# Interaction tower on one core: gathered rows turned by DMAs instead of on TensorE, sums in smaller groups, and a table load that waits piece by piece

## What is computed

```python
e = jnp.stack([tbl_f[ids[:, f]] for f in range(32)], axis=1)      # 2048 x 32 x 64
z = jnp.sum(e, axis=-1)
outer = jnp.einsum('bpd,pde,bpe->bp', e[:, II, :], kernels, e[:, JJ, :])
h = jnp.concatenate([z, outer, dense_ctx], axis=1)
h = jnp.maximum(h @ W_top1 + b_top1, 0.0)
h = jnp.maximum(h @ W_top2 + b_top2, 0.0)
y = h @ W_top3
```

## Time and profile before

| | |
|---|---|
| median of 3 runs (range) | 1235.91 us (1235.64 to 1238.09) |
| the profiled execution | 1238.17 us |
| its span, first to last instruction | 1236.4 us |
| TensorE matmul busy | 1074.5 us, 87% |
| VectorE (DVE) busy | 628.0 us, 51% |
| ScalarE (ACT) busy | 142.5 us, 12% |
| GpSimd (POOL) busy | 483.8 us, 39% |
| mean granted TensorE clock | 0.945 of full speed |

### The profile page before, as it was taken

One profiled execution on the slowest core, in us unless ns is written; L12 is line 12 of the kernel. 1 busy time (PEld: TensorE's weight loads), 2 busy tenths in 40 slices (PEclk: granted clock), 3 DMA queues, 4 the chain that ended last, 5 costly groups with the idle time before them and its releaser, 6 DMA issues.

```text
span 1236.4 us, 30329 instructions
## 1 busy us (share of the span) xinstructions
PE 1074.5 (87%) x13964; PEld 460.2 (37%) x13964; DVE 628.0 (51%) x658; ACT 142.5 (12%) x219; POOL 483.8 (39%) x518
## 2 busy tenths in 40 slices
PE   1565737898989888999999999989998999999998
PEld 0453614343334233334343443333343343333333
DVE  0331412264546353656665654556664655589880
ACT  0100110101001101201010021210020020210101
POOL 7444373325543443454445433354445423400000
PEclk9877768899989789999999999999999999999999
DMA  9100010001010000010010000000011000000000
GB/s 335 38 17 18 16 26 13 15 11 21 19 22 12 16 17 14 15 21 18 17 20 20 18 13 13 15 19 19 19 19 20 19 10 15 16 3 2 3 3 0
DMA packets 24376, 29.24 MB, mean 24 GB/s; under 512 B 13366, under 2 KB 13624, under 8 KB 24123
## 3 DMA queue, kind: packets, MB, share of 16 engines
q0 software_dynamic: 16384, 16.81, 7.0%
q1 hardware_dynamic: 7856, 10.49, 2.5%
q10 hardware_dynamic: 10, 0.01, 0.0%
HBM read 27.27 MB, written 0.01 MB: 22 GB/s over the span
## 4 chain that ended last, share of the span: by engine, by line
PE 85%; issue 11%; DVE 1%; another core or an unknown queue 1%; DMA 1%; POOL 1%; ACT 0%; DVEq 0%; ACTq 0%; POOLq 0%
PE y L631 48%; PE accs L649 25%; PE y L611 3%; PE y L710 2%; PE y L693 2%; PE y L681 2%; DVE prod L576 1%; PE y L686 1%; PE y L723 1%; POOL rows L384 1%; DMA rows<-tbl,ids_sb 0%; ACT xt L430 0%; PE y L662 0%; DMA ids_sb<-ids 0%
## 5 line engine op out<-in xcount | busy, mean ns | idle before, releaser
L576 DVE TENSOR_TENSOR prod<-y,xt 128x1024 f32<-128x1024 f32 (+3 forms) x570 | 587.5, 1080 | 561.9 <-PE y L631 373.3
L384 POOL DMA_INDIRECT rows<-tbl,ids_sb x512 | 483.1, 944 | 597.3 <-DVE prod L576 309.2
L631 PE MATMUL y<-xt,kw 64*32 64x512 f32 (+2 forms) x8432 | 647.8, 560 | 66.9 <-issue 53.0
L649 PE MATMUL accs<-prod,ones_strip 64*32 64x512 f32 (+2 forms) x4960 | 352.5, 526 | 67.5 <-issue 66.6
L631 PEld LDWEIGHTS y<-xt,kw 64*32 64x32 f32 (+1 forms) x8432 | 236.8, 115 | 422.5 <-issue 384.4
L649 PEld LDWEIGHTS accs<-prod,ones_strip 64*32 64x32 f32 x4960 | 149.0, 112 | 232.2 <-issue 208.2
L430 ACT COPY xt<-y 128x1024 f32<-128x1024 f32 (+2 forms) x48 | 34.9, 728 | 608.0 <-PE y L611 513.0
L611 PE MATMUL y<-ident,rows 128*128 128x128 f32 x256 | 42.3, 289 | 21.4 <-DMA rows<-tbl,ids_sb 16.2
L548 DVE TENSOR_REDUCE z_rows<-rows 128x8 f32<-128x512 f32 (+2 forms) x80 | 42.9, 570 | 15.2 <-DMA rows<-tbl,ids_sb 15.2
L611 PEld LDWEIGHTS y<-ident,rows 128*128 128x128 f32 x256 | 28.7, 142 | 49.8 <-issue 42.7
L461 ACT COPY h_in<-accs 128x1024 f32<-128x1024 f32 (+2 forms) x10 | 8.4, 842 | 221.1 <-PE accs L649 141.4
(11 more groups left out here) (22 smaller groups left out, 67.5 us busy)
## 6 DMA issues: line engine op xcount, KB each, us to landing
rows<-tbl,ids_sb POOLq DMA_INDIRECT x512
kw<-pair_k SPq DMA_DIRECT2D x14, 512.0 KB
w_sb<-w SPq DMA_DIRECT2D x1, 1024.0 KB
w_sb<-w SPq DMA_DIRECT2D x1, 512.0 KB
kw<-pair_k SPq DMA_DIRECT2D x1, 384.0 KB
kw<-pair_k SPq DMA_DIRECT2D x1, 256.0 KB, 4.1
w1z_sb<-w1z SPq DMA_DIRECT2D x1, 256.0 KB
ids_sb<-ids SPq DMA_DIRECT2D x1, 240.0 KB, 2.7
```

The lines of the kernel that those rows point to most:

```text
L384: pool.indirect_dma_start(out=rows[:, s, c, h, :], out_offset=None, in_=tables[f], in_offset=bass.IndirectOffsetOnAxis(ap=ids_sb[:, b, f:f ...
L576: nc.vector.tensor_tensor(prod_part(t, d, n), y_part(t, d, n), x, ALU.mult).then_inc(y_read, n)
L631: last = nc.tensor.matmul(y[columns, h, :], kw[part, d, columns], xt[part, slot_of(t, units[h][0] // 2), 0:w], start=True, stop=True)
L649: last = nc.tensor.matmul(accs[32 * q:32 * q + 32, n, 0:w], ones_strip[part, STRIPS - 1 - s:2 * STRIPS - 1 - s], prod_part(t, u // 2)[part ...
```

## The change

It has three parts.

**Rows turned by DMAs.** In tiles 1 to 4 TensorE no longer transposes. A float32 is two 16-bit halves. ACT copies a couple's gathered rows apart into low and high halves (`split_rows`, new buffer `split`), SP issues one transposing DMA for the couple from `split` to `halves`, and ACT copies the halves together into `xt` (`join_halves`). The transposing DMAs go one at a time, and two couples can be on the way. `join_at` and `split_at` take the place of `visits`: a couple is joined three full steps before the first step that needs it and at least 2.5 before the next couple's join, and split five full steps ahead of its join. Gathers start 48 full steps ahead of the split. A row slot is free when the couple has been split and summed. To make room, `xt` has 18 slots instead of 20 and `h2` lies in `h1`. Tile 0 is turned on TensorE as before. The dense columns go through ACT's queue into one of two buffers, and the field sums are turned at step 108 of each tile instead of 76.

**Sums.** Groups are two `prod` slots, four groups are in flight, and sums go two groups behind.

**The table.** Each of the 17 DMAs waits until the one before it has landed (the first six), later until the one before that has.

```diff
-XT_SLOTS = 20
+XT_SLOTS = 18
+HALF_SLOTS = 2
 FIRST_EXTRA = XT_SLOTS
 EXTRAS = 4
 Y_SLOTS = 3
-GROUP_SLOTS = [4] * TILES
+GROUP_SLOTS = [2] * TILES
+PROD_GROUPS = 4
+SUM_LAG = 2
...
+K_ALONE = 6
...
-def visits_ahead(t):
-    return {1: [(0, 112), (2, 116)], 2: [(0, 100), (2, 112)]}.get(t, [(0, 84), (2, 100), (4, 116)])
-def visits(t):
-    early = {1: [(4, 4), (6, 14), (8, 26), (10, 44)], 2: [(4, 2), (6, 12), (8, 24), (10, 40)]}
-    return early.get(t, [(6, 8), (8, 20), (10, 36)]) + [(12, 56), (14, 72)]
+JOIN_MARGIN = 3
+JOIN_SPACING = 2.5
+JOIN_LEAD = 5
+FIRST_SPLITS = [(0, 100), (0, 104), (0, 110), (0, 116), (1, 1), (1, 4), (1, 9), (1, 14), (1, 20)]
+FIRST_JOINS = [(0, 108), (0, 112), (0, 120), (0, 123), (1, 4), (1, 8), (1, 13), (1, 18), (1, 24)]
+def full_steps(t, d):
+    return (N_STEPS * sum(WIDTHS[:t]) + d * WIDTHS[t]) / TILE
+def join_at(t, k):
+    if t == 1 and k < len(FIRST_JOINS):
+        return full_steps(*FIRST_JOINS[k])
+    d = first_step_of_couple(k) if k < COUPLES - 1 else step_at("inner", SETS - 1, 0) - 6
+    at = full_steps(t, d) - JOIN_MARGIN
+    return at if k == COUPLES - 1 else min(at, join_at(t, k + 1) - JOIN_SPACING)
+def split_at(t, k):
+    if t == 1 and k < len(FIRST_SPLITS):
+        return full_steps(*FIRST_SPLITS[k])
+    return join_at(t, k) - JOIN_LEAD
+def moves_of(t):
+    moves = {d: [] for d in range(N_STEPS)}
+    events = [(at(u, k), what, u, k) for u in range(1, TILES) for k in range(COUPLES)
+              for what, at in (("split", split_at), ("join", join_at))]
+    for at, what, u, k in sorted(events):
+        if full_steps(t, 0) <= at < full_steps(t, N_STEPS):
+            moves[int((at - full_steps(t, 0)) * TILE / WIDTHS[t] + 1e-6)].append((what, u, k))
+    return moves
...
-    for k, d in visits(t):
-        work[d // p * p].append(("couples", t, k))
-    work[76].append(("fields", t, 0))
-    if t + 1 < TILES:
-        for k, d in visits_ahead(t + 1):
-            work[d // p * p].append(("couples", t + 1, k))
...
-            if g > 0:
-                order.append(("sum", t, g - 1))
+            if g >= SUM_LAG:
+                order.append(("sum", t, g - SUM_LAG))
             elif t > 0:
-                order.append(("sum", t - 1, len(groups(t - 1)) - 2))
+                order.append(("sum", t - 1, len(groups(t - 1)) - 1 + g - SUM_LAG))
...
-GATHER_LEAD = 56
-STEPS_BEFORE = {}
-_steps = 0
-for _what in PLAN:
-    STEPS_BEFORE[_what] = _steps
-    _steps += _what[0] == "step"
+GATHER_LEAD = 48
...
-    what = Y_ORDER[copy_use(t, k)]
-    goal = FULL_STEPS[STEPS_BEFORE[what]] - GATHER_LEAD + i + 2 * rowsets(t) * (k - what[2])
+    goal = split_at(t, k) - GATHER_LEAD + i
...
+        split = sb("split", [P, HALF_SLOTS, 2 * TILE // P, P], u16)
+        halves = sb("halves", [P, HALF_SLOTS, 2 * TILE // P, P], u16)
...
-        h2 = sb("h2", [P, J2, TILE])
+        h2 = h1[:, 0:J2, :]
...
-            slot = PROD_SLOTS // 2 * (group_number(t, d) % 2) + i // pack(t)
+            slot = GROUP_SLOTS[t] * (group_number(t, d) % PROD_GROUPS) + i // pack(t)
...
-                        pool.wait_ge(y_full, copy_use(*divmod(n - GATHER_SLOTS, COUPLES)) + 1)
+                        before, kb = divmod(n - GATHER_SLOTS, COUPLES)
+                        if before == 0:
+                            pool.wait_ge(y_full, y_use("couple", 0, kb) + 1)
+                        else:
+                            pool.wait_ge(rows_split, move_number(before, kb) + 1)
...
+                if c >= 1:
+                    sp.wait_ge(k_loaded[c - (1 if c < K_ALONE else 2)], 16)
...
-            sp.wait_ge(z_rows_zeroed, 1)
-            for t in range(TILES):
-                if t > 0:
-                    sp.wait_ge(y_full, y_use("fields", t - 1, 0) + 1)
-                for half in range(2):
-                    sp.dma_start(z_rows[:, 0:rowsets(t), half, FIELDS:FIELDS + DENSE],
-                                 dense[:, first_block(t):first_block(t) + rowsets(t), :]).then_inc(dense_loaded, 16)
+            for t in range(1, TILES):
+                for k in range(COUPLES):
+                    i = move_number(t, k)
+                    slot, r = i % HALF_SLOTS, 2 * rowsets(t)
+                    sp.wait_ge(rows_split, i + 1)
+                    if i >= 1:
+                        sp.wait_ge(transposed, 16 * i)
+                    if i >= HALF_SLOTS:
+                        sp.wait_ge(joined, i - HALF_SLOTS + 1)
+                    sp.dma_start_transpose(halves[:, slot, 0:r, :],
+                                           split[:, slot, 0:r, :].rearrange("p c d -> p (c d)")
+                                           ).then_inc(transposed, 16)
...
+            def load_dense(t):
+                for half in range(2):
+                    act.dma_start(z_rows[:, t % 2, 0:rowsets(t), half, FIELDS:FIELDS + DENSE],
+                                  dense[:, first_block(t):first_block(t) + rowsets(t), :]
+                                  ).then_inc(dense_loaded[t % 2], 16)
...
+            def split_rows(t, k):
+                n, i, r = couple(t, k), move_number(t, k), 2 * rowsets(t)
+                words = rows[:, n % GATHER_SLOTS, 0:rowsets(t), :, :].rearrange("p c h d -> p (c h d)").bitcast(u16)
+                act.wait_ge(gathered[n % GATHER_SLOTS], rows_in(n))
+                if i >= HALF_SLOTS:
+                    act.wait_ge(transposed, 16 * (i - HALF_SLOTS + 1))
+                nc.scalar.copy(split[:, i % HALF_SLOTS, 0:r, :].rearrange("p (s c) d -> p s (c d)", s=2),
+                               words.rearrange("p (n s) -> p s n", s=2)).then_inc(rows_split, 1)
+            def join_halves(t, k):
+                n, i, r, w = couple(t, k), move_number(t, k), 2 * rowsets(t), WIDTHS[t]
+                act.wait_ge(transposed, 16 * (i + 1))
+                if n >= XT_SLOTS:
+                    before, kb = divmod(n - XT_SLOTS, COUPLES)
 
                     act.wait_ge(y_read, N_STEPS * before + last_step_of_couple(kb) + 1)
-                s = slot_of(t, k)
-                nc.scalar.copy(xt[:, s:s + count, 0:w], y_banks[u % Y_SLOTS][:, 0:count, 0:w]).then_inc(act_read, 1)
+                nc.scalar.copy(xt[:, slot_of(t, k), 0:w].bitcast(u16).rearrange("p (n s) -> p s n", s=2),
+                               halves[:, i % HALF_SLOTS, 0:r, :].rearrange("p (s c) d -> p s (c d)", s=2)
+                               ).then_inc(joined, 1)
...
-                if g >= 2 and d in groups(t):
-                    dve.wait_ge(summed, g - 1)
+                if g >= PROD_GROUPS and d in groups(t):
+                    dve.wait_ge(summed, g - PROD_GROUPS + 1)
...
-                pe.wait_ge(act_read, copied(t, max(units[0][0], units[1][0]) // 2))
+                k = max(units[0][0], units[1][0]) // 2
+                if t == 0:
+                    pe.wait_ge(act_read, act_uses_through(y_use("couple", 0, k)))
+                else:
+                    pe.wait_ge(joined, move_number(t, k) + 1)
```

More of the change, by code:

```diff
@@ L161, in first_tile_work @@
         work[d // p * p].append(("extra", 0, s))
-    for k, d in visits_ahead(1):
-        work[d].append(("couples", 1, k))
     work[108].append(("fields", 0, 0))
@@ L205 @@
 PLAN = [what for t in range(TILES) for what in plan(t)]
-Y_ORDER = [what for what in PLAN if what[0] not in ("sum", "extra") and (what[0] != "step" or what[2] % pack(what[1]) == 0)]
+Y_ORDER = [what for what in PLAN if what[0] in ("couple", "fields", "mlp1", "mlp2", "mlp3")
+           or what[0] == "step" and what[2] % pack(what[1]) == 0]
 Y_USES = {what: u for u, what in enumerate(Y_ORDER)}
```

104 lines of the change are left out of this document (54 added, 50 removed).

## The result

| | before | changed |
|---|---|---|
| median, range | 1235.86 (1235.64 to 1238.09) | 1257.56 us (1252.67 to 1260.91) |
| ratio, 95% interval | | 1.0165 [1.0144, 1.0185] |
| profiled execution, its span | 1238.17, 1236.4 | 1260.91, 1259.1 us |
| mean granted clock | 0.945 | 0.905 |

Slower by 21.7 us, where the forecast was slower by 7.6.

A forecast was written before the change was run, and what follows sets the result against it. TensorE sets the end, held up by gathers that are cheap spread and dear bunched. 1238.2 - 70.8 + 82 + 0 - 3.6 = 1245.8 us profiled, 1243.5 us median; forecast 1215 to 1275, whole range 1194 to 1296.

The forecast's parts named there:

- transposes leave TensorE: Tiles 1 to 4: turning rows by DMAs takes the transposes off TensorE, -70.8 us, or -56.4 at the lower price.
- gathers bunched: Gathers for tiles 2 to 4: the new order adds 102 back-to-back gathers at 0.80 us each, +82 us.
- smaller groups: Sums: smaller groups keep the step-to-sum distance, move no work and remove a DVE wait that ends last nowhere, 0.
- transposing DMAs: Row turning in tiles 1 to 4: DMAs arrive in time and their traffic is taken as 0, up to +24 us.
- table in pieces: Start of the kernel: loading the table in pieces removes POOL's stand, -3.6 us, with ends 0 and -16.
- 48 x (6.33 - 5.15): Tiles 2 to 4: 48 couples times 1.18 us for eight transposes each on TensorE, 56.6 us.
- rival (3): Tiles bound by gathers: transposes were already paid for in part, 0.94 instead of 1.18 us; 1258 us, within the forecast's 0.48.
- doubled gathers: Gathers sharing a full step with another instead of having their own; 102 more after the change, 0.80 us each.
- with at most two pieces on the way that goes: Tile 0's start: TensorE's stand from 20.05 to 36.22 us behind the table load disappears.
- (1): Gathers: bunching costs less, below 0.73 us per doubled gather, so the kernel is faster; 1202 us at 0.40; chance 0.29.
- (2): Tiles 2 to 4: slow transposing DMAs deliver halves late or their traffic holds up matmuls; 1292 us; chance 0.20.
- tiles 3 and 4 no shorter than before: Sign of being right: these two tiles would not get shorter after the change.

The follow-up runs named there:

- e13: Kernel before with small groups of sums and the changed kernel's gather times in tiles 2 to 4, where before takes 1236.6 to 1237.1: 1267.52 us, 1.0241.
- e4: Kernel before with only the small groups: two product slots, four groups in flight, sums two groups behind: 1210.03 us, 0.9787.
- e16: Changed kernel with 46 of the 64 transposing DMAs replaced by plain 4 KB DMAs, copies, waits and order kept: 1256.94 us, 1.0152.
- e3: Kernel before with only the waits between the 17 DMAs of the table: 1237.06 us, 1.0004.
- e15: Kernel before with small groups of sums and even gather times in tiles 2 to 4, rows turned on TensorE: 1162.37 us, 0.9402.
- e17: Kernel before with only the even gather times in tiles 2 to 4, on a chip where before takes 837.84: 837.49 us, 0.9992.
- e12: Kernel before with small groups and the changed kernel's gather times in tiles 2 to 4, where before takes 837.3 to 837.8: 831.93 us.
- e1: Changed kernel with gathers of tiles 2 to 4 let go evenly, one per full step: 1152.82 us, 0.9325.
- e18: Changed kernel with even gathers six steps earlier and a short POOL MEMSET after each gather of tiles 1 to 4, where before takes 837.84: 881.55 us, 1.0516.

## Why the prediction came out as it did

The direction was right and the time inside the range, but both by luck, and the size was not right: +7.6 us forecast, +21.7 measured, made of three terms that were each off by 24 us or more. By its own terms, on holding chips:

| term | forecast | measured | from |
|---|---|---|---|
| transposes leave TensorE | -70.8 | -9.9, the DMAs and the pieces with it | e13 to changed |
| gathers bunched | +82 | +57.5 | e4 to e13 |
| smaller groups | 0 | -26.5 | before to e4 |
| transposing DMAs | 0 | 0 (0.6) | e16 |
| table in pieces | -3.6 | 0 (+0.5) | e3 |
| sum | +7.6 | +21.1 | the first three |

The three are steps of one path, before to e4 to e13 to changed, so that they add up to the whole is no proof of them; by another path they share it differently.

**The step that failed first is "48 x (6.33 - 5.15)".** The row shows eight transposes, the code says eight *gathers* a couple, and I took the one for the other; a couple of a wide tile has four transposes. The term was 35.4 us at most. With the right count the forecast would have been 1279 us, further off, because the other errors would not have made it up.

**The second is that 1.18 us was carried into cycles with gathers.** The forecast had a row against it (0.94) and a rival (3), "the transposes were paid for in part already". That rival was right, and far stronger than its 0.94: of 35.4 us, 9.9 were got. By tiles from e13 to the changed kernel: tile 2 0.2 us and tile 3 1.6; tile 4, where three of five visits are free of gathers, 3.9; tile 1 5.6; tile 0 5.2 longer, after a start 3.1 us earlier. Where gathers hold nothing up the price holds, as tiles 2 to 4 on the free chip show. That the rest was hidden in stands is shown only in part, as said at e15.

**The third is "take away a wait of DVE that ends last nowhere: 0" for the smaller groups.** Its reasoning looked at waits, and the gain lies in tiles 2 and 3, where TensorE stands beside gathers and the profile names no wait. The 26.5 us are shown; by what path they come is not. Small groups gave 32 us beside TensorE's transposes in the bunched order (1299.5 to 1267.5), 26.5 in the kernel before's, and 2.8 where DMAs turn, so the two edits may take away the same stands. But the 2.8 were measured in the even order and the others not, so it may as well be that order which leaves small groups nothing to gain. The run that would have told (e17) met a free chip. What is measured for the two together is 41.9 us, in the bunched order (1299.5 to 1257.6).

**The bunching** was right in place, and in size for two tiles. For tiles 2 and 3 the forecast had 40 doubled gathers x 0.80 = 32 us each; from e4 to e13 they grew by 32.3 and 31.1. It was wrong at the edges: tile 1, forecast at +17.6, became 6.5 us shorter, since its gathers fell from 120 to 112 (column POOL), and tile 4, which had no term, got those 8 more and took 5.3 us longer. (The tiles add up to 62.0 us, for the profiled executions; the medians differ by 57.5.) Two things the forecast did not have. One is the clock. In e13 tiles 2 and 3 were granted 0.94 and 0.95 of it, in e4 1.00. Estimated from these rows, TensorE lost at most 17 of the 32 us and 15 of the 31 by that, if it had worked all the while; how much it really lost, no run tells. The other is where gathers lie: 22 of them moved out of tile 1 go with 43.1 us (e4 to e15), 1.96 each, which is above the 1.25 us that the forecast had as its upper end.

**The table in pieces** brought TensorE's first step of tile 0 forward by 3.3 us in e3's trace, and the medians don't show it. The changed kernel still has this stand at the start, beside gathers:

```profile
L704 PE MATMUL y<-xt,kw 64*32 64x512 f32 (+2 forms) x8432 | 775.1, 574 | 92.5 <-issue 79.3 <-ACT xt L467 8.2 <-ACT xt L488 1.6
```

(its 79.3 us of "issue" contain one of 11.4 from 18.4 to 29.8 us, while the table comes in pieces). In e3 that first stand is gone and a later one of 12.1 us comes in its place. So "with at most two pieces on the way that goes" failed as an account of the time: the load was not alone what TensorE stood behind in the earlier trace rows.

**Of the rivals**, (1) was right in its number, 0.56 us for a doubled gather (57.5 / 102) and below its bound of 0.73, and wrong in its outcome, because the other side of the sum was smaller still. (2), late halves or traffic, is refuted by 4.67 us a move and by e16.

**What "wrong" rows missed.** I had named cycles, runs and waits that would show the mechanisms. All came as written but one: tile 4 is 3.5 us shorter, where "tiles 3 and 4 no shorter than before" was a mark of being right. None of them checked a count, and the count alone was 35.4 of the 60.9 us by which the largest term was off.

## What to carry to other kernels

Before a price is multiplied, tie the count in the row to the count in the code by a total (256 transposes in the page, not 48 times eight). Where an engine stands for a cause that overlaps its work, terms don't add: work taken off it there may be worth nothing (0.0 to 0.3 us in each of two tiles, against 9 to 11 where nothing stands), so price it in stretches with the stand and without. And an order of gathers tuned on one chip can be worth 8% there (1257.6 to 1152.8 us) and 0.2% on another (807.5 to 806.2): the even order was the better or equal one on both. Before a gain is put down to an order's evenness, count per tile: here most of it went with gathers that had moved to another tile.

## What the runs showed of the hardware

The same program takes 1237 us on three chips and 838 on three others, steadily on each, with the same 5.15 us for four steps without gathers and the same 1.25 us between gathers. The difference is TensorE's stand by "issue" beside indirect DMAs from POOL: 7.5 us for a cycle with four gathers against 5.15. In the wide tiles it goes with the gathers: e13 and e12 are one program, and its tiles 2 and 3 take 287.2 and 293.3 us on a holding chip against 191.2 and 195.7 on a free one, but tile 4, with 40 gathers on the first, 208.4 against 193.7. It shows at the steps and sums, which come in many small records; the perceptron's 16 matmuls took 7.13 us in e1 with two gathers started beside them (from 702.46 us) and 7.03 without (from 1137.09), on a holding chip. What differs between the chips no view shows; instruction packets take about as long on both (median 1.07 us in the trace of the kernel before, 0.98 in e12's). Whether gathers set further apart would hold up less on a holding chip was to be seen in e18 and is open.

A transposing DMA of eight 128x128 blocks of 16-bit numbers is through in under 4.7 us, and replacing 46 of them by DMAs of 4 KB changed the kernel's time by 0.6 us, which is noise. The Trainium skill ("Advanced Engine Details and Errata", section "X-Bar Transpose (TRN2)") says they run as fast as plain ones, and the trace agrees roughly: 3.07 to 4.67 us with the issue, against 2.6 and 4.1 us for a plain one of 256 KB.
